# Negated score maxima added by eight-row products in row tiles, in place of two DMAs into the operand

## The reference

```python
x = x + tanh(g_xattn[0]) * xattn(layernorm(x), ctx, Wq, Wkv_expand, Wout)
# inside xattn, per sequence and head (256 x 256 scores):
scores = einsum('bhqd,bhkd->bhqk', qh, kh) / sqrt(32)
scores = where(causal, scores, finfo.min)
attn = softmax(scores, axis=-1)          # subtracts each query's maximum
out = einsum('bhqk,bhkd->bhqd', attn, vh)
# then the feed-forward block
x = x + tanh(g_ffn[0]) * ffn(layernorm(x), w_gate_up, w_down)
```

## Time and profile before

| | |
|---|---|
| Median of 2 runs | 912.08 us (911.38 to 912.78) |
| Profiled execution, own time | 911.37 us |
| Its span in the profile | 909.6 us |
| Mean granted TensorE clock | 0.953 of 2.4 GHz |

### The profile page before, as it was taken

The page is one execution under the profiler, slowest core; times in us unless marked ns, Lnnn a source line. Parts: engine busy times, 40 slices in busy tenths (PEclk is TensorE's granted clock), DMA queues, the critical chain, the costliest instruction groups (busy, mean ns, idle before and its releaser), DMA issues. The chain is left out here.

```text
span 909.6 us, 19898 instructions
## 1 busy us (share of the span) xinstructions
PE 805.3 (89%) x6491; PEld 585.9 (64%) x6520; DVE 649.8 (71%) x2029; ACT 460.0 (51%) x728; POOL 517.7 (57%) x671
## 2 busy tenths in 40 slices
PE   3569999998999989989999999886799999999995
PEld 2458787776777877777778768665345555555552
DVE  3573786786776757867768657646688988888882
ACT  5325546546456365464554562432255555555552
POOL 4524457456366364573654753531467777777774
PEclk9678999999999999999999999898799999999998
DMA  6775658577495593774954944434102222222222
GB/s 210 173 177 133 166 138 214 130 188 179 109 239 139 127 238 105 182 201 103 223 146 126 254 108 106 128 111 187 47 18 88 88 88 87 88 87 89 84 78 94
DMA packets 75814, 124.51 MB, mean 137 GB/s; under 512 B 27456, under 2 KB 38208, under 8 KB 75456
## 3 DMA queue, kind: packets, MB, share of 16 engines
q1 hardware_dynamic: 74688, 122.72, 50.8%
q10 hardware_dynamic: 1024, 0.53, 0.3%
HBM read 47.06 MB, written 25.30 MB: 80 GB/s over the span
## 5 line engine op out<-in xcount | busy, mean ns | idle before, releaser
L655 DVE CUSTOM_DVE_ANT_0 junk<-psum,mask 128x128 f32<-128x128 f32 (+1 forms) x512 | 159.7, 354 | 17.2 <-PE psum L844 15.3
L1190 PE MATMUL psum<-w1q,xqb 128*128 128x512 bf16 (+1 forms) x752 | 163.0, 365 | 4.9 <-DVE gate L1133 2.2
L391 POOL TENSOR_SCALAR_AFFINE_SELECT prob<-prob 128x512 f32<-128x512 f32 x128 | 79.9, 635 | 88.0 <-ACT prob L589 87.2
L1190 PEld LDWEIGHTS psum<-w1q,xqb 128*128 128x128 bf16 x768 | 74.3, 99 | 79.3 <-issue 8.3
L1072 POOL TENSOR_TENSOR up<-gate,up 128x512 f32<-128x512 f32 (+1 forms) x96 | 111.9, 1182 | 9.0 <-DVE up L1138 9.0
L589 ACT ACTIVATE prob<-psum 128x768 f32<-128x768 f32 x128 | 100.6, 820 | 12.5 <-PE psum L913 12.3
L1104 ACT ACTIVATE up<-up,round_bias,hinv 128x1408 f32<-128x1408 f32 x32 | 50.0, 1561 | 99.8 <-DVE hinv L1157 99.8
L911 PE MATMUL psum<-qs,ks 98*128 98x256 f32 x256 | 76.6, 360 | 18.2 <-ACT prob L589 11.4
L1212 PE MATMUL psum<-w2q,hqT 128*128 128x512 bf16 x339 | 82.1, 388 | 0.7
L842 PE MATMUL psum<-ks,qs 96*128 96x128 f32 x256 | 66.7, 261 | 17.0 <-DMA qs<-q_lo 12.0
L440 POOL TENSOR_TENSOR o_lo<-u,o_hi 128x512 fp32r<-128x512 f32 x32 | 41.2, 1289 | 68.5 <-ACT o_hi L537 68.5
(11 more groups left out here) (130 smaller groups left out, 2023.0 us busy)
## 6 DMA issues: line engine op xcount, KB each, us to landing
ks<-k_hi SPq DMA_DIRECT2D x128, 128.0 KB, 3.7
qs<-q_hi SPq DMA_DIRECT2D x128, 128.0 KB, 4.7
xln<-x_dram SPq DMA_DIRECT2D x16, 512.0 KB, 5.4
ks<-k_lo SPq DMA_DIRECT2D x64, 128.0 KB, 3.4
qs<-q_lo SPq DMA_DIRECT2D x64, 128.0 KB, 4.4
x<-x_dram SPq DMA_DIRECT2D x16, 512.0 KB, 4.9
x_scratch<-x SPq DMA_DIRECT2D x16, 512.0 KB, 5.1
x1b<-x_scratch SPq DMA_DIRECT2D x32, 256.0 KB, 2.7
```

Of the source, the lines that this page charges most:

```text
L391: pool.affine_select(out=blk, in_=blk, compare_op=ALU.is_ge, fill=0.0, base=0, pattern=[[0, 4], [1, P]], channel_multiplier=-1).then_inc(s ...
L655: dve.tensor_tensor_reduce(junk[:, n % 2, 0:w], psum[:, h % 4, cols], m, 1.0, LOWEST, ALU.add, ALU.max, mx[:, par, t, h:h + 1]).then_inc(s ...
L1190: last = pe.matmul(psum[:, (2 * r + n) % 4, 0:w], xqb[:, r, k, :], w1q[:, k, half * I + o:half * I + o + w], start=(k == 0), stop=(k == KH ...
```

## The change

Rows 96 and 97 are gone from `qs` and `ks` (K = 96), and with them the two DMAs of each slot (32 in all), the semaphore `m_moved`, and the two settings of ones (L729). `nm` becomes 128 columns wide, mostly zero: group j of four heads has its high parts in columns 32j to 32j+3 and its low parts in 32j+4 to 32j+7, written by four VectorE operations instead of two. TensorE transposes 128 x 128 instead of 128 x 32, so `nmT` has the parts of group j at rows 32j to 32j+7. After the two products of each of its two heads, `score_pair` adds four products with eight rows: the weights are `sel[rows, g]` (ones in the two rows of head g, all 128 columns), the moving operand is `nmT[rows]`, 256 and then 128 columns. The two heads of a pair lie in different groups of 32 rows and go to different banks. `sel` is made once, in slot -1. TensorE now waits for ScalarE's copy (`mt_copied`) instead of the DMAs. To make room, the small statistics tiles are put into one tile `small`, and `rec_hi` shares `rec2`.

```diff
-        nm = inA("nm", [P, ST, 2, NHEAD], F32R)
-        nmT = inA("nmT", [2 * NHEAD, S], F32R)
+        nm = inA("nm", [P, ST, P], F32R)
+        sel = inA("sel", [P, GROUPS, P], F32R)
+        nmT = inA("nmT", [P, S], F32R)
@@ ScalarE
                         act.wait_ge(s["mt_done"], b + 1)
-                        wait_for(act, s["m_moved"], 2 * DMA * b)
-                        act.activation(nmT[:], psum[0:2 * NHEAD, 0, 0:S], ACT.Copy).then_inc(s["mt_copied"], 1)
-                        act.wait_ge(s["mt_copied"], b + 1)
-                        wait_for(act, s["st_done"], PAIRS * (b - 1))
-                        for part in range(2):
-                            act.dma_start(qs[3 * HD + part:3 * HD + part + 1, par, :, :].bitcast(F32),
-                                          nmT[NHEAD * part:NHEAD * (part + 1), :].bitcast(F32)).then_inc(s["m_moved"], DMA)
+                        wait_for(act, s["st_done"], PAIRS * b)
+                        act.activation(nmT[:], psum[:, 0, 0:S], ACT.Copy).then_inc(s["mt_copied"], 1)
@@ VectorE
-                        dve.tensor_scalar(nm[:, :, 0, :], mx[:, par, :, :], -1.0, None, ALU.mult).then_inc(s["nm_hi"], 1)
-                        dve.wait_ge(s["nm_hi"], b + 1)
-                        dve.scalar_tensor_tensor(out=nm[:, :, 1, :], in0=mx[:, par, :, :], scalar=-1.0,
-                                                 in1=nm[:, :, 0, :].bitcast(F32), op0=ALU.mult,
-                                                 op1=ALU.subtract).then_inc(s["nm_lo"], 1)
+                        parts = nm[:].rearrange("p t (j w) -> p t j w", w=HD)
+                        for t in range(ST):
+                            dve.tensor_scalar(parts[:, t, :, 0:GROUPS], mx[:, par, t, :].rearrange("p (j g) -> p j g", g=GROUPS),
+                                              -1.0, None, ALU.mult).then_inc(s["nm_hi"], 1)
+                        dve.wait_ge(s["nm_hi"], 2 * b + 2)
+                        for t in range(ST):
+                            dve.tensor_tensor(parts[:, t, :, GROUPS:2 * GROUPS], mx[:, par, t, :].rearrange("p (j g) -> p j g", g=GROUPS),
+                                              parts[:, t, :, 0:GROUPS].bitcast(F32), ALU.add).then_inc(s["nm_lo"], 1)
-                    if isinstance(b, int) and -1 <= b < 1:
-                        dve.memset(ks[3 * HD:3 * HD + 2, 1 - par, :, :].bitcast(F32), 1.0).then_inc(s["ones_set"], 1)
@@ TensorE, score_pair
-                        K = 3 * HD + 2
+                        K = 3 * HD
                         for d in range(2):
                             h, bank = GROUPS * (j + d) + g, 2 * (pair % 2) + d
                             early = psum[:, bank, 0:CAUSAL].rearrange("p (k q) -> p k q", q=P)[:, 0:3:2, :]
                             pe.matmul(early, ks[0:K, par, h, 0:P], qs[0:K, par, h, 0:S].rearrange("p (k q) -> p k q", q=P),
-                                      start=True, stop=True)
-                            last = pe.matmul(psum[:, bank, P:S], ks[0:K, par, h, P:S], qs[0:K, par, h, P:S],
-                                             start=True, stop=True)
+                                      start=True, stop=False, skip_group_check=True)
+                            pe.matmul(psum[:, bank, P:S], ks[0:K, par, h, P:S], qs[0:K, par, h, P:S],
+                                      start=False, stop=False, skip_group_check=True)
+                        for d in range(2):
+                            rows, bank = slice(HD * (j + d), HD * (j + d) + 2 * GROUPS), 2 * (pair % 2) + d
+                            pe.matmul(psum[:, bank, 0:S], sel[rows, g, :], nmT[rows, :],
+                                      start=False, stop=True, skip_group_check=True)
+                        for d in range(2):
+                            rows, bank = slice(HD * (j + d), HD * (j + d) + 2 * GROUPS), 2 * (pair % 2) + d
+                            last = pe.matmul(psum[:, bank, S:CAUSAL], sel[rows, g, :], nmT[rows, P:S],
+                                             start=False, stop=True, skip_group_check=True)
                         last.then_inc(s["st_done"], 1)
@@ TensorE, slot
-                            last = pe.transpose(psum[0:2 * NHEAD, 0, t * P:(t + 1) * P],
-                                                nm[:, t, :, :].rearrange("p a h -> p (a h)").bitcast(F32), ident[:])
+                            last = pe.transpose(psum[:, 0, t * P:(t + 1) * P], nm[:, t, :].bitcast(F32), ident[:])
-                        pe.wait_ge(s["m_moved"], 2 * DMA * (b + 1))
+                        if b == 0:
+                            pe.wait_ge(s["sel_set"], 3 + GROUPS)
+                        pe.wait_ge(s["mt_copied"], b + 1)
                     score_pair(0)
```

More of the change, by code:

```diff
@@ L160, in gated_block @@
         wintT = inA("wintT", [P, IT, P], BF16)
-        wmax = inA("wmax", [P, 2], F32)
-        wstep = inA("wstep", [P, 2], F32)
-        winv = inA("winv", [P, 2], F32)
         st1 = inA("st1", [P, ST, 6], F32)
[L165 to L168, removed]
+        small = inA("small", [P, 16, ST], F32)
         st2 = inA("st2", [P, ST, 6], F32)
[L170 to L176, removed]
+        ve1, rs1, nb1, ve2, rs2, nb2, am2, sx2, ri2, wmax, wstep, winv = (small[:, i, :] for i in range(12))
+        mv1, mv2 = small[:, 12:14, :], small[:, 14:16, :]
+        sel_col, sel_sign = junk[:, 0, 0:GROUPS], junk[:, 1, 0:1]
         wq_raw = v[:].rearrange("p a t h -> p (a t) h")
@@ L676, in slot @@
                         dve.wait_ge(s["rec_done"], b)
-                        dve.tensor_copy(rec_hi[:], rec[:]).then_inc(s["rec_hi"], 1)
+                        wait_for(dve, s["bc_done"], 2 * tb)
+                        dve.tensor_copy(rec2[:], rec[:]).then_inc(s["rec_hi"], 1)
                         dve.wait_ge(s["rec_hi"], b)
-                        wait_for(dve, s["bc_done"], 2 * tb)
-                        dve.scalar_tensor_tensor(out=rec2[:], in0=rec_hi[:].bitcast(F32), scalar=lo_rows[:, 0:1],
+                        dve.scalar_tensor_tensor(out=rec2[:], in0=rec2[:].bitcast(F32), scalar=lo_rows[:, 0:1],
                                                  in1=rec[:], op0=ALU.mult, op1=ALU.add).then_inc(s["rec_split"], 1)
@@ L726, in slot @@
                         dve.tensor_reduce(lo_rows[:], lo_tab[:], AX.X, ALU.add).then_inc(s["table"], 1)
-                    if isinstance(b, int) and -1 <= b < 1:
-                        dve.memset(ks[3 * HD:3 * HD + 2, 1 - par, :, :].bitcast(F32), 1.0).then_inc(s["ones_set"], 1)
+                        dve.memset(nm[:].bitcast(F32), 0.0).then_inc(s["sel_set"], 1)
+                        dve.tensor_reduce(sel_col, spread_f.rearrange("p (g c) -> p g c", g=GROUPS), AX.X,
+                                          ALU.max).then_inc(s["sel_set"], 1)
+                        dve.wait_ge(s["table"], 4)
+                        dve.tensor_scalar(sel_sign, lo_rows[:], 2.0, 1.0, ALU.mult, ALU.add).then_inc(s["sel_set"], 1)
+                        dve.wait_ge(s["sel_set"], 3)
+                        for g in range(GROUPS):
+                            dve.scalar_tensor_tensor(out=sel[:, g, :], in0=ones[:], scalar=sel_col[:, g:g + 1],
+                                                     in1=sel_sign.to_broadcast([P, P]), op0=ALU.mult,
+                                                     op1=ALU.mult).then_inc(s["sel_set"], 1)
                     def residual(t):
@@ L902, in score_pair @@
                         g, j = pair // 2, 2 * (pair % 2)
-                        if isinstance(b, int) and b < 2 and pair == 0:
-                            pe.wait_ge(s["ones_set"], b + 1)
                         if pair >= 2:
                             pe.wait_ge(s["exp_done"], PAIRS * b + pair - 1)
-                        K = 3 * HD + 2
+                        K = 3 * HD
                         for d in range(2):
@@ L980, in slot @@
                     if present(b):
[L981 removed]
+                        pe.wait_ge(s["nm_lo"], 2 * b + 2)
                         for t in range(ST):
[L983 to L984 removed]
+                            last = pe.transpose(psum[:, 0, t * P:(t + 1) * P], nm[:, t, :].bitcast(F32), ident[:])
                         last.then_inc(s["mt_done"], 1)
```

8 lines of the change are left out of this document (3 added, 5 removed).

## The result

| | before | after |
|---|---|---|
| median, us | 912.08 (911.38 to 912.78) | 951.65 (948.99, 954.31) |
| ratio | | 1.0433 [1.0393, 1.0474] |
| profiled execution, us | 911.37 (span 909.6) | 954.31 (span 952.6) |
| granted clock, mean | 0.953 | 0.93 |

What follows compares the result with a forecast made beforehand. TensorE, busy 89%, was taken as the bound, with the q loop setting 11 slots; 12.8 + 7.4 - 3.6 gave +16.6 us on 911.37, 928.0, rounded down to 927 us, range 908 to 946.

Steps and rivals of the forecast that it cites:

- The sum of a slot: Slots behind slot 0: added products lengthen 11 slots that wait for q by 1.16 us each, four others by 1.84.
- rival D: Score pairs: changes of tiling are nearly free and the clock comes back, 910 us (905 to 919); chance 0.18.
- A: Score pairs: the two heads' row tiles run side by side; the forecast itself, 924 to 930 us; chance 0.42.
- b: Time of a pair's four added products without changes of tiling: taken as 0.30 us, bounded by 0.23 and 0.47.
- X: Added time of a pair that goes back to untiled products: b plus 0.28 for changes of tiling, 0.58 us.
- rival B: Score pairs: the row tiles don't run side by side, b is 0.47 us, the kernel takes 944 us; chance 0.25.
- Rival C: Score pairs: a change into or out of row tiles costs double, 0.56 for 0.28 us; 950 us; chance 0.08.
- The delay of `transposed_q(1)`: Pairs 0 and 1 delay it by 1.16 us, which lengthens the 11 slots that wait for q by as much.
- G: TensorE's own growth in a slot: 0.16 before pair 2, 3.03 for pairs 2 to 7, less 1.35 slack: 1.84 us.
- Slot 0: Its 5.18 us wait goes: 3.2 us back, 1.5 from the clock, less 2.0 for new products: -2.7 us.
- What was removed: Waits for the maxima's DMAs: -2.7 us in slot 0, new products included, and -0.9 elsewhere, -3.6 in all.
- VectorE's part: Four operations in place of two ahead of the transposes add about 0.2 us, costing 0 to 0.4 in all.

Runs made afterwards that it cites:

- the execution of 929: The profiled run of the unedited changed kernel timed again in a second set: 929.34 us; that set's median was 951.21 us.
- experiment 2: Changed kernel with the 512 added products left out, transposes, VectorE's part and copy kept: 905.92 us, 0.9950 of the kernel before.
- experiment 4: Changed kernel with the added products on 32 rows of their tile instead of 8, the 24 others zero: 928.06 us, 1.0178 of the kernel before.
- experiment 7: Changed kernel with 32 rows and each head's added products directly behind its own, four tiling changes a pair instead of two: 1074.67 us, 1.1774.
- 10: Changed kernel with one untiled 128-row product of 384 columns a head, plus `transposed_q(1)` moved ahead of pair 0: 914.95 us, 1.0040 of the kernel before.
- 9: Kernel before with `transposed_q(1)` moved from behind pair 1 to ahead of pair 0: 902.69 us, 0.9924.

## Why the prediction was wrong

The step that failed is none of the sums but what they rest on. "The sum of a slot" prices every pair at full clock and takes the score phase to stay there; the only words on the clock are of its return (the 1.5 us in slot 0, rival D). The earlier trace rows had shown a score phase, slot 0's, at 0.50 for 8.21 us with TensorE busy for 8.16 of them. I read it as the echo of the wait before, though the row itself says that 8 us of score products without a gap did not bring the clock up. That the added products could take it down was no rival.

Set against the fourteen slots behind slot 0, the 42.9 us divide so: the kernel before took 494.86 us for them, with 32 rows and the clock at 1.00 it is 510.33, the changed kernel took 537.78. So 15.5 us are the change at full clock and 27.4 the fall of the clock (the changed kernel's own slots at full clock, in the execution of 929, took 506.64, which would make it 11.8 and 31.1). That it is the added products is shown by experiment 2, that it is neither their time nor the tiling alone by 4. What decides, and is shown, is how many rows of a tile are in use (8, 16, 32: 950, 934, 927.5 us, medians of 16, 4 and 10 runs). It rests on tiles with two changes a pair alone. The order of the products counts as well (with 32 rows a mean clock of 0.966 in experiment 4, 0.87 in 7), but whether by the changes of tiling or by the thinner use of the array is open. Why the clock falls around pair 2, and in which slots and executions, is not explained: the kernel is the same in 929 and in 962 us.

*At full clock, point by point.*

- *The total*: forecast +16.6. With 32 rows it is +16.5 (926.7 against 910.2). The likeliest case, A, was right for a kernel that keeps its clock, but by luck, for two errors cancel: in the profile of experiment 4 slot 0 ends 0.4 us later than before, where 2.7 less were forecast, and the fourteen slots behind it cost 15.5, where the sum has 18.3 (11 x 1.16 + 3 x 1.84) less the 0.9 of small waits.
- *b and X*: the block was taken as 0.30 and the changes as 0.13 and 0.16, X = 0.58. Measured, a pair behind a change grew from 0.46 to 0.98 (1.04 was forecast), so X = 0.52. Row and drain can't be told apart within the block (0.22 for the two products of 256 columns, 0.15 for the other two and the change behind them). If b is what one head's two products take untiled, 0.22, the changes take 0.30, near the 0.28 that I had, and it was b = 0.30 that was too high.
- *Side by side or not (rival B)*: experiment 7 settles it, one tile and two take the same 0.23 and 0.15 us. The rule of the Trainium skill ("TensorE: Matmul & The Clock Gate", Part 3, the mechanism), that a load runs beside a product of another row group, would have made b near 0.23, and the trace agrees in that the second tile's loads and products add no time. So does the other rule cited ("TensorEngine Tiling (Array Packing)", Key Properties), that a change of mode drains the engine: the same products cost 1.50 us a pair with four changes and 0.98 with two, of which about 0.2 (an estimate, a head's two untiled products) is the end of the work side by side. Rival C's time, 950, is next to the result and B's, 944, not far, and neither mechanism is there: the changes cost about what I had.
- *The delay of `transposed_q(1)`* was put at 1.16, and the slots that wait for q at 36.7 us. Two pairs cost 0.41 and 0.52, so 0.93; the eleven slots that end in this wait with 32 rows have a median of 36.66. That this loop sets them is shown by 10, where the move takes 11.1 of 11.3 us of waiting away, and less clearly by 9.
- *G, TensorE's own growth*, was 1.84. In slots 1 and 13, which end without a wait for q before and in experiment 4, that shows 0.51 (35.22 against 34.71) and 1.55 (35.65 against 34.10). So more than the 1.35 us of slack that I read gives way; where, I did not trace. The q wait so stays at 10.9 us in 11 slots with 32 rows, where near 0.4 each was forecast.
- *Slot 0* was to give 2.7. The wait went, pair 0 started at 62.75 us and pair 2 at 66.81 (70.23 before), yet the next slot starts at 84.83 against 85.38. The gain of 3.4 us was used up behind it, at half clock (0.60 from 66.81 to 76.42 us), where the added products cost double. The 1.5 us of clock return did not come: from pair 0 on the clock was 0.50 for 11.7 us (62.75 to 74.47), before for 8.3 (68.21 to 76.49).
- *What was removed* gives 5.7 us without the products (experiment 2). The forecast's 3.6 has 2.0 of slot 0's new products taken off, so it says 5.6. The products then cost 22.2 us (928.1 - 905.9), and the forecast is the same, 20.2 and these 2.0. With the two errors above this too is in part luck.
- *VectorE's part*: the wait of the transposes for it is 3.4 us, 3.1 of them in slot 0 (60.98 us), against 3.1 before. Small, as forecast.

On the clock, the trace shows TensorE busy for 21.12 us of 21.12 at a granted 0.52, with no gap ahead. The Trainium skill ("TensorE: Matmul & The Clock Gate", HAM oscillation) puts the loss of the clock down to idle gaps between groups of products; by that rule this phase would have kept it, and here the measurement decides. The same page of the Trainium skill (A second HAM failure mode) has a kernel in which the clock swings because TensorE idles very briefly between groups. The drains at the changes of tiling could be such moments, and experiment 7 speaks for it; experiment 4, with the same changes as the changed kernel and no fall, says that they are not the whole of it. No row of products shows idle time within a change, but their ends are modelled. The weight loads do stand still there, at full clock for 0.07 us (287.71 to 287.78):

```profile
287.52 0.19 PEld L905 LDWEIGHTS psum<-qs,ks 96*128 96x128 f32 x1
287.78 0.18 PEld L909 LDWEIGHTS psum<-nmT,sel 8*128 8x128 f32 x2
```

Whether that bears on the clock stays open.

## What to carry to other kernels

Before small products are put between dense ones, read what clock the stretch is granted now, and ask what a fall would cost: here 7 to 8 us more for each of three slots, against 1.1 us for the products. If a product needs only a few rows, try full tiles or the whole array with zeros in it, and collect the tiles so that the tiling changes in and out once; rows cost nothing in time (a pair takes 0.98 us with 8, 0.97 with 32). And look at what sets the period first: the loop through `transposed_q(1)` and one DMA in slot 0 were worth 11 us with one line moved and two added, twice what the removal of every wait for the maxima was.

## What the runs showed of the hardware

- The granted clock fell to its lower level and stayed there for 17 to 21 us, in seven slots of four profiles, with TensorE busy throughout, in score phases with products of 8 rows in two row tiles between K = 96 products. Each fall came 3.2 to 3.8 us behind pair 0; with 32 rows in the same tiles it stayed at 1.00 for 510 us.
- With 32 rows it fell too when each head's products stood by themselves (four changes of tiling a pair in place of two, one row tile at a time): 0.86 over 627 us, with TensorE busy for 619 of them.
- The second row tile of a pair costs nothing: 0.23 and 0.15 us for one head or for two. A pair with one change in and one out takes 0.97 us in place of 0.46.
- A selector of one column that is read 128 times as weights is as fast as weights laid out: the four added products take 0.45 us with it (178.32 to 178.77), two heads' K = 96 products of the same columns 0.46. The pair takes 0.86 us, 0.82 with one product of 384 columns a head, and the clock stays (mean 0.965 and 0.968).
